# Row-centred output weights, and a sum of squares on ScalarE, for the two output LayerNorms of an attention and slot-mixture kernel

## What is computed

```python
def _layernorm(x, axis=-1, eps=1e-05):
    m = jnp.mean(x, axis=axis, keepdims=True)
    v = jnp.var(x, axis=axis, keepdims=True)
    return (x - m) / jnp.sqrt(v + eps)
...
x = x + _layernorm(_L0_attn_ref(_layernorm(x), ...))   # ends in  out @ Wo + bo
x = x + _layernorm(_L0_ffn_ref(_layernorm(x), ...))    # ends in  out @ c_Wo + c_bo
```

## Time and profile before

| | |
|---|---|
| median of 3 runs | 501.3 us (497.4 to 502.04) |
| the profiled execution, its own time | 501.44 us |
| its span, first to last instruction | 499.4 us |
| PE busy, of the span | 403.0 us (81%) |
| DVE busy | 308.8 us (62%) |
| ACT busy | 232.0 us (46%) |
| POOL busy | 149.2 us (30%) |
| mean granted TensorE clock | 0.919 |

### The profile page before, as it was taken

One profiled execution on the slowest core, in us unless ns is written; L12 is line 12 of the kernel. 1 busy time (PEld: TensorE's weight loads), 2 busy tenths in 40 slices (PEclk: granted clock), 3 DMA queues, 4 the chain that ended last, 5 costly groups with the idle time before them and its releaser, 6 DMA issues.

```text
span 499.4 us, 6939 instructions
## 1 busy us (share of the span) xinstructions
PE 403.0 (81%) x2072; PEld 249.7 (50%) x2072; DVE 308.8 (62%) x1177; ACT 232.0 (46%) x422; POOL 149.2 (30%) x253
## 2 busy tenths in 40 slices
PE   3876657569799955759899999999996679999981
PEld 3533223225455532545677675834442326888871
DVE  4599999979995948253542534333332214969984
ACT  2326646747768656456765564200000001356765
POOL 3105554465755350311330220010000000335453
PEclk9997887979799977688999999999998879999997
DMA  4293011001010261217545676639999999801223
GB/s 146 81 315 107 1 43 42 19 24 43 1 42 3 74 252 43 78 53 266 209 148 174 219 233 219 257 140 402 387 399 388 397 378 354 266 0 43 84 86 126
DMA packets 43599, 81.69 MB, mean 164 GB/s; under 512 B 1831, under 2 KB 36269, under 8 KB 39085
## 3 DMA queue, kind: packets, MB, share of 16 engines
q1 hardware_dynamic: 42504, 80.05, 45.7%
q10 hardware_dynamic: 1060, 1.22, 0.8%
HBM read 69.73 MB, written 11.53 MB: 163 GB/s over the span
## 4 chain that ended last, share of the span: by engine, by line
PE 53%; DVE 20%; ACT 8%; issue 5%; SPq 5%; DMA 4%; POOL 3%; DVEq 1%; POOLq 0%; ACTq 0%
PE bank L1469 6%; PE bank L1445 6%; PE bank L1112 5%; PE bank L1078 5%; PE bank L1141 5%; PE bank L1045 4%; DVE top L1608 4%; SPq L403 4%; PE bank L1358 4%; DMA x<-in_L_ffn_e_W_dram 3%; PE bank L1067 3%; DVE exc L1639 2%; DVE stats L1533 2%; PE bank L1057 2%; PE bank L1388 2%
## 5 line engine op out<-in xcount | busy, mean ns | idle before, releaser
L1045 PE MATMUL bank<-Wz,yT 128*128 128x512 f32 x128 | 70.7, 704 | 24.2 <-DVE top L1608 21.6
L1045 PEld LDWEIGHTS bank<-Wz,yT 128*128 128x128 f32 x128 | 28.2, 229 | 60.4 <-issue 49.2
L1608 DVE MAX8 top<-bank 128x8 f32<-128x32 f32 x512 | 51.5, 180 | 4.1 <-ACT scr L727 2.4
L979 ACT ACTIVATE d<-d 128x32 f32<-128x32 f32 x16 | 3.7, 229 | 92.1 <-DVE d L1959 92.1
L1078 PE MATMUL bank<-aWo,hoT 128*128 128x256 f32 x128 | 39.4, 434 | 3.5 <-DVE arena L1727 3.5
L568 POOL TENSOR_SCALAR veps<-mv 128x4 f32<-128x4 f32 x24 | 5.7, 237 | 110.4 <-DVE mv L1536 83.3
L675 POOL TENSOR_TENSOR work<-work 128x512 f32<-128x512 f32 x16 | 16.6, 1060 | 64.7 <-DVE work L2024 64.7
L1727 DVE TENSOR_TENSOR arena<-bank,Wz 128x256 f32<-128x256 f32 x16 | 6.7, 418 | 45.1 <-PE bank L1078 45.1
L706 ACT ACTIVATE arena<-arena,shift,rstd 128x256 f32<-128x256 f32 x64 | 33.2, 596 | 2.6 <-POOL shift L690 2.6
L1067 PE MATMUL bank<-heads 128*64 128x256 f32 x128 | 22.9, 437 | 11.4 <-issue 5.8
L1078 PEld LDWEIGHTS bank<-aWo,hoT 128*128 128x128 f32 x128 | 23.7, 205 | 14.1 <-issue 10.2
(11 more groups left out here) (256 smaller groups left out, 877.9 us busy)
## 6 DMA issues: line engine op xcount, KB each, us to landing
x<-in_L_ffn_e_W_dram SPq DMA_DIRECT2D x9, 1024.0 KB, 9.9
arena<-in_L_ffn_e_W_dram SPq DMA_DIRECT2D x9, 1024.0 KB, 13.8
scr<-in_L_ffn_e_W_dram SPq DMA_DIRECT2D x8, 1024.0 KB, 14.6
arena<-in_L_ffn_e_Wg_dram SPq DMA_DIRECT2D x6, 1024.0 KB, 6.9
work<-in_L_ffn_e_W_dram SPq DMA_DIRECT2D x5, 1024.0 KB, 8.4
xin<-in_L_attn_query_dram SPq DMA_DIRECT2D x8, 512.0 KB, 4.1
x<-in_L_attn_query_dram SPq DMA_DIRECT2D x1, 4096.0 KB, 16.5
out_dram<-x SPq DMA_DIRECT2D x8, 512.0 KB, 3.2
```

What stands on the lines that cost most here:

```text
L1045: mm = pe.matmul(bZ[t % 2][:, :], yT[:, c, t * P:(t + 1) * P], Wz[:, c, :], start=(c == 0), stop=(c == C - 1))
L1608: mx = v.max(top[:, h * TG + t, :], bZ[t % 2][:, h * NS:(h + 1) * NS])
```

## The change

The columns of the output weights `aWo` and `cWo` and of the output biases are centred once: from each row of 256 values its mean is taken away. The projection then has mean zero over its 256 outputs, so the norm needs the mean square alone, and no shift.
- ACT centres with `centre_rows`, two activations for each row block, the second of which waits for the first: `aWo` (two blocks) and `cbo` right after the loop over groups 0 and 1, ahead of `clamp(2)`; `abo` ahead of `signs(7, 1)`; `cWo` (two blocks) after the experts' last Silu. DVE centres `bo3` with three small instructions ahead of `split3`.
- `output_statistics` and `norm_out` (DVE), `norm_o` and `apply_out` (ACT) go. For the first batch ACT follows each `take_o(n)` by a Square of the tile with a sum over the row; in the last stage `square_out(j)`, four Squares, follows `put_out(j)`. Each Square waits for the one before it and for ACT's own copy. The second batch's heads keep DVE's statistics.
- The Square of the first tile of a group waits in addition for POOL to have read the sums of the group before: `vare[1]` at g.
- POOL's `roots(1, g)` and `out_roots` have two instructions where they had four.
- `join` and `add_stream` have one SCALAR_TENSOR_TENSOR for each tile (scale times output plus x) where one TENSOR_TENSOR added the whole group, and wait for POOL in place of ACT.

```diff
+                if k == 1 and i < GB:
+                    pool.tensor_scalar(veps[:, k, :], osq[:, :], 1.0 / D, EPS, ALU.mult, ALU.add).then_inc(vare[k], 1)
+                else:
+                    pool.tensor_scalar(veps[:, k, :], mv[:, k, :, 1], EPS, None, ALU.add).then_inc(vare[k], 1)
+                if k == 1:
+                    pool.wait_ge(vare[k], i + 1)
+                    pool.tensor_tensor(rstd[:, k, :], veps[:, k, :], mhalf[:, :], ALU.pow).then_inc(rst[k], 1)
+                    return
...
                 act.activation(o[:, g % 2, n % TG, :], psO, ACT.Copy).then_inc(o_sb, 1)
-
-            def norm_o(g, tiles=range(TG)):
-                act.wait_ge(rst[1], g + 1)
-                for t in tiles:
-                    scaled(1, t, o[:, g % 2, t, :], o[:, g % 2, t, :]).then_inc(o_norm, 1)
+                if n % TG == 0 and g >= 1:
+
+                    act.wait_ge(vare[1], g)
+                if n > 0:
+                    act.wait_ge(mean[1], n)
+                act.wait_ge(o_sb, n + 1)
+                act.activation(unread[:, :], o[:, g % 2, n % TG, :], ACT.Square, accum_out=osq[:, n % TG:n % TG + 1])\
+                    .then_inc(mean[1], 1)
+
+            def centre_rows(k, rows_, idle):
+
+                act.activation(idle, rows_, ACT.Identity, scale=-1.0 / D, accum_out=centre[:, k:k + 1]).then_inc(summed, 1)
+                act.wait_ge(summed, k + 1)
+                act.activation(rows_, rows_, ACT.Identity, bias=centre[:, k:k + 1]).then_inc(centred, 1)
...
+            act.wait_ge(w_in1, 16 * N_W1)
+            act.wait_ge(bo_in, 32)
+            for c in range(C):
+                centre_rows(c, aWo[:, c, :], hoT[:, 0, :, :].rearrange("p m n -> p (m n)"))
+            centre_rows(2, cbo[:, :], hoT[:, 0, :, :].rearrange("p m n -> p (m n)"))
             clamp(2)
...
             take_o(15)
+            act.wait_ge(abo_in, 16)
+            centre_rows(3, abo, Wz[:, 0, D:2 * D])
             signs(7, 1)
...
+            act.wait_ge(w_in3, 16 * N_W3)
+            for c in range(C):
+                centre_rows(4 + c, cWo[:, c, :], y[:, 2, :])
...
+            def square_out(j):
+                k0 = next(k for k, p in enumerate(portions) if p[0] == j)
+                for t in range(TG):
+                    k = k0 if t < portions[k0][2] else k0 + 1
+                    if k >= 3 and t == portions[k][1]:
+
+                        act.wait_ge(c_vare, k - 2)
+                    if j * TG + t > 0:
+                        act.wait_ge(c_mean, j * TG + t)
+                    act.wait_ge(co_sb, j * 2 + (t // 2 + 1))
+                    act.activation(unread[:, :], co[j % CO][:, t, :], ACT.Square, accum_out=csq[:, k % 3, t:t + 1])\
+                        .then_inc(c_mean, 1)
...
                 put_cpT(j)
-                if j >= 2:
-                    apply_out(j - 2)
                 put_out(j)
-            for k in range(NG - 2, len(portions)):
-                apply_out(k)
+                square_out(j)
...
             def join(g):
-                v.wait_ge(o_norm, g * TG + TG)
-                tiles = x[:, g * TG:(g + 1) * TG, :]
-                v.tensor_tensor(tiles, tiles, o[:, g % 2, :, :], ALU.add).then_inc(x_new, 1)
+                v.wait_ge(rst[1], g + 1)
+                for t in range(TG):
+                    tile = x[:, g * TG + t, :]
+                    x_ = v.scalar_tensor_tensor(out=tile, in0=o[:, g % 2, t, :], scalar=rstd[:, 1, t:t + 1], in1=tile,
+                                                op0=ALU.mult, op1=ALU.add)
+                x_.then_inc(x_new, 1)
```

More of the change, by code:

```diff
@@ L124, in build @@
         cbo = sb("cbo", [P, D])
+        centre = sb("centre", [P, 6])
+        osq = sb("osq", [P, TG])
+        csq = sb("csq", [P, 3, TG])
+        unread = sb("unread", [P, D], BF16)
         stats = sb("stats", [P, 3, TG, 6])
@@ L225, in build @@
         bo_in = sem("bo_in")
+        summed = sem("summed")
+        centred = sem("centred")
         w_in2 = sem("w_in2")
@@ L683, in out_roots @@
                 if k >= 3:
[L684 to L690, removed]
+                    hold(c_out, k - 2)
+                pool.tensor_scalar(veps[:, w, lo:hi], csq[:, w, lo:hi], 1.0 / D, EPS, ALU.mult, ALU.add).then_inc(c_vare, 1)
+                pool.wait_ge(c_vare, k + 1)
+                pool.tensor_tensor(rstd[:, w, lo:hi], veps[:, w, lo:hi], mhalf[:, lo:hi], ALU.pow).then_inc(c_rst, 1)
             weigh(0, 0)
@@ L921, in _ @@
             put_slot_scores(1)
-            norm_o(2)
             take_h(15)
@@ L961, in _ @@
             second_norm(6)
-            norm_o(7)
             put_norm(6)
@@ L1013, in _ @@
             put_out(0)
+            square_out(0)
             for j in range(1, NG):
@@ L1074, in project @@
                     pe.wait_ge(o_sb, n)
+                else:
+                    pe.wait_ge(centred, C)
                 if n < KT:
@@ L1425, in fold_values @@
             def fold_values(b):
+                pe.wait_ge(centred, 6)
                 for m in range(2):
@@ L1714, in check @@
                 v.tensor_copy(flag[:, :], moved[:, 0:1]).then_inc(settled, 1)
[L1716 to L1722, removed]
             def keep_output(n):
@@ L1847, in _ @@
             v.wait_ge(bo_in, 32)
+            bsum = centre[0:3, 4:5]
+            own(v.tensor_reduce(bsum, bo3, AX_X, ALU.add))
+            own(v.tensor_scalar(bsum, bsum, 1.0 / D, None, ALU.mult))
+            own(v.tensor_scalar(bo3, bo3, bsum, None, ALU.subtract))
             own(split3(ab3[:, :], bo3))
@@ L1891, in _ @@
             check(1)
-            output_statistics(3)
             group_maximum(1)
-            v.wait_ge(abo_in, 16)
+            v.wait_ge(centred, 4)
             for n in range(KT + 2, 2 * KT + 2):
@@ L2024, in total @@
                     v.reciprocal(crs[:, half], csum[:, half]).then_inc(c_rs, 1)
[L2026 to L2039, removed]
-                    v.bn_aggr(mv[:, w, t, :], stats[:, w, t, :]).then_inc(c_mean, 1)
             def add_stream(k):
@@ L2044, in add_stream @@
                 v.wait_ge(back[j % 2], 16 * (j // 2 + 1))
-                v.wait_ge(c_norm, j * TG + hi)
-                tiles = co[j % CO][:, lo:hi, :]
-                v.tensor_tensor(tiles, tiles, x[:, j * TG + lo:j * TG + hi, :], ALU.add).then_inc(c_out, 1)
+                v.wait_ge(c_rst, k + 1)
+                for t in range(lo, hi):
+                    tile = co[j % CO][:, t, :]
+                    c_ = v.scalar_tensor_tensor(out=tile, in0=tile, scalar=rstd[:, k % 3, t:t + 1], in1=x[:, j * TG + t, :],
+                                                op0=ALU.mult, op1=ALU.add)
+                c_.then_inc(c_out, 1)
             soften(0, 0)
```

19 lines of the change are left out of this document (1 added, 18 removed).

## The result

Slower, as forecast, and by somewhat more. The changed kernel has a median of 510.8 us (507.5 to 511.0, 4 runs) beside 499.4 us for the kernel before on the same chip, a ratio of 1.023 [1.018, 1.028]. A second series gave 510.9 us (508.4 to 512.8, 6 runs) beside 497.6 (17 runs), 1.026 [1.023, 1.029]. I had said 509, from +8.0 on the profiled execution's 501.44. The profiled executions differ by 9.2 us (510.61 and 501.44; spans 508.8 and 499.4); the medians differ by 11 to 13, since that profiled execution lay near the upper end of the kernel before's runs (495.7 to 503.2 in all series).

The account below looks back on a forecast made before the run. It took ACT as the awaited engine early on and PE as busy throughout from 425 to 475 us. +5.3 us up to 290 us and +2.7 in the last stage made +8.0 on 501.44: 509 us, 8-in-10 range 501 to 516.

Parts of the forecast that it names:

- (1): Ahead of clamp(2): three centring pairs on ACT lie on the path, +2.9 us (2.1 to 3.4).
- (2): bo3 centred on DVE, about 1.1 us: hidden by DVE's wait for ACT's scores, 0; +1.1 without that cover.
- (8): cWo centred on ACT after the last Silu, 1.9 us: hidden behind PE's remaining work, 0.
- (3): First batch's heads: DVE's saved statistics gain 0; Squares of tiles 3, 8 and 13 delay awaited work, +0.6, +0.6, +0.5 us.
- (4): Tile 12's Square waits for POOL on vare[1]: ACT stands still 5 us and take_o(13) ends later, +0.5 us.
- (6): Joins 0 to 7 each take 0.3 us longer; joins 1, 2, 4 and 6 are on the path, +1.2 us.
- (7): norm_o(3) gone: join(3) starts 1.3 us sooner but takes 0.3 more, -1.0 us; later norm_o's gone give 0.
- (9): Last stage: rounds 8.01 us for 7.78, +1.15; outputs(6) and outputs(7) +2.2 each; end -2.8; sum +2.7 us.
- A: Rival: ACT's Squares cost nearly nothing, 0.35 us each with overlap kept, giving 504.4 us; chance 0.15.
- B: Rival: DVE's relief at the four output_statistics counts, 7.2 us off the path, giving 496.5 or 494 us; chance 0.09.
- C: Rival: PE's pauses drop the granted clock for a tenth of the last stage's 75 us, 7 us more, 516 us; chance 0.12.
- D: Rival: Square needs another activation table, 18 us or more of loads in the last stage, 527 us; chance 0.04.

Follow-up runs that it names:

- experiment 2: Kernel before with only the last stage changed (square_out after put_out) and cWo and cbo centred after the last Silu: 503.16 us, ratio 1.006.
- experiment 8: Kernel before with only the last stage's change, square_out(j - 1) after put_cpT(j), last group's first two Squares between put_out's halves: 493.04 us, ratio 0.992.
- experiment 10: Kernel of experiment 8 plus 8 idle matmuls ahead of the products of experts 11 to 15: 493.53 us, ratio 0.993 to the kernel before.
- experiment 3: Changed kernel with square_out(j - 1) moved behind put_cpT(j), same instructions: 503.54 us, ratio 1.010 to the kernel before.
- experiment 5: The changed kernel timed again, unaltered, as measure for other runs: 510.9 us, ratio 1.026 to the kernel before.
- experiment 6: Changed kernel with 12 idle matmuls ahead of outputs(6) and 9 ahead of outputs(7): 508.88 us, ratio 1.023 to the kernel before.
- experiment 9: Changed kernel with 8 idle matmuls ahead of the products of experts 11 to 15: 508.05 us, ratio 1.020 to the kernel before.
- experiment 7: Changed kernel with aWo and cbo centred early, Squares behind put_cpT, and two sets of sums avoiding the POOL wait: 502.36 us, ratio 1.010 to the kernel before.
- experiment 1: Changed kernel with the last stage, cWo and cbo as before, so the first norm's half alone: 505.96 us, ratio 1.014 to the kernel before.
- experiment 4: Changed kernel with aWo and cbo centred between put_yT(0) and norm_y(1), ahead of the loop: 509.37 us, ratio 1.020 to the kernel before.
- experiment 11: Changed kernel with the three centring pairs ahead of clamp(2) made twice: 513.68 us, ratio 1.033 to the kernel before.
- experiment 12: Changed kernel with two sets of sums, so tile 12's Square no longer waits for POOL: 510.05 us, ratio 1.024 to the kernel before.

## Why the prediction was right, point by point

The direction and the places were right; up to 290 us the terms come to +5.2 for +5.3 once traces of like clock are compared, and the clock, which I had kept as a rival, made part of the time behind. For the heads every trace is cut at the same matmuls of PE; times that name a stretch are those of the kernel before.

A profiled pair alone doesn't price them. The kernel before and experiments 2, 8 and 10 run the same program up to the experts, and so do the changed kernel and experiments 3, 5, 6 and 9. And executions of one program still differ: at the matmul that ends the gathering the first four stand at 288.26, 288.55, 288.80 and 283.81 us, the other five at 291.87, 294.49, 293.21, 290.16 and 290.48. So the 3.6 us of the profiled pair there is one draw, and what an edit costs has to be read between traces whose granted clock is the same in that stretch (numbers in brackets are those of experiments, "all ten" with the half counts the changed kernel):

| stretch, and what is in it | without the first norm's half | with it | difference |
|---|---|---|---|
| 64.1 to 80.5, centring | 16.44 (before) | 19.26 (experiment 3); 16.44 where it is moved (7) | +2.82 |
| 110.2 to 131.8, tile 3, clock 1.00 | 21.60 (before, 2, 8) | 22.20 (3, 7) | +0.60 |
| the same, low clock in the first 3 to 4 us | 21.17 (10) | 21.77 (1, 4, 6, 9) | +0.60 |
| 213.9 to 218.9, `join(3)` | 4.97 (all four) | 4.00 (all ten) | -0.97 |
| 237.9 to 242.0, `join(4)` | 4.14 (all four) | 4.59 (1, 6, 9, 11) | +0.45 |
| 259.9 to 288.3, `join(6)` | 28.37 (all four) | 28.80 (all ten) | +0.43 |

The clock in two of these pairs: windows (us; PE, PEld, DVE, ACT, POOL busy; clock; DMA share, GB/s) of the kernel before and of experiment 3, which was 0.6 us later up to 71 us and has 0.57 from 67.6 to 71.6 us as the kernel before has from 67 to 71:

```profile
74.00:78.00 4.00, 3.31 (x5) 1.55 (x6) 3.54 (x23) 3.97 (x5) 2.88 (x5) 0.57 0.00 0
110.00:132.00 22.00, 18.31 (x86) 10.55 (x86) 21.28 (x118) 15.69 (x29) 13.41 (x13) 1.00 0.08 25
```

```profile
74.60:78.60 4.00, 3.29 (x5) 1.53 (x6) 2.13 (x22) 3.90 (x12) 2.90 (x5) 0.57 0.00 0
114.00:136.00 22.00, 18.08 (x84) 10.27 (x81) 21.29 (x118) 16.96 (x36) 13.40 (x13) 1.00 0.09 25
```

(1) Centring, +2.9: 2.82 us at 0.94 for a pair (I had 0.95), and experiment 11 and the first row of the table show it on the path. In the profiled run only 1.8 show at 80 us, since the clock from 65 to 75 us happened to be higher than before (1.00 against 0.74 and 0.84).

(2), (5) and (8), priced at nothing, cost nothing that the traces show; for `cWo` experiment 2 shows it, while no run has (2) or (5) alone.

(3) The Squares in the heads, forecast +0.6, +0.6 and +0.5. Tile 3's costs its 0.60 (table). The profiled pair can't show it: the ten traces with the half spread from 21.77 to 22.72 us there with the clock. Tile 8's and `join(1)` show at the end of their stage: 170 to 182 us takes 11.55 us in the four kernels without that half and 12.61 to 12.63 in all ten with it, +1.07 where I had +0.9. Ahead of `clamp(7)` the Square takes its 0.42 us behind `take_o(13)`.

(4) The wait for POOL, +0.5: 0.1 (experiment 12). The mechanism was exact, a stop of 5.90 us where I had said 5; I had set too much work behind it.

(6) The joins: 0.45 us longer each, not 0.3 (1.67 against 1.22). From 182 to 202 us, where tile 13's Square, the wait and `join(2)` together were +1.3, the traces have 21.15 against 20.33, +0.8.

(7) `norm_o(3)` gone, -1.0, with `join(4)` and `join(6)`, +0.6: -0.4 forecast for 202 to 288 us. By the table it is -0.97 + 0.45 + 0.43, so -0.1: the gain was exact, the joins longer. The whole stretch shows the clock more than this: it takes 87.8 us in the changed kernel and 87.0 to 87.8 in experiments 3, 4, 5, 7 and 12, 84.8 to 85.3 in experiments 1, 6, 9 and 11, and 85.9 in the kernel before, but 85.1 in experiment 10. The first six have a granted clock of 0.83 from 240 to 250 us, and all others 1.00. Windows of the changed kernel and of experiment 9:

```profile
240.00:250.00 10.00, 8.11 (x38) 6.07 (x39) 4.77 (x19) 5.17 (x9) 3.96 (x10) 0.83 0.30 118
```

```profile
240.00:250.00 10.00, 7.93 (x47) 5.82 (x47) 5.01 (x20) 6.19 (x12) 3.96 (x10) 1.00 0.57 208
```

Without what the clock did, (1) to (7) thus come to 2.8 + 0.6 + 1.1 + 0.8 - 0.1 = +5.2, for +5.3. The changed kernel's own trace has +3.6 at 288 us, from larger pieces of both signs: 132 to 142 us took 7.2 us in place of 9.9, at a clock that had been low before (0.83 from 130 to 150 us) and was 1.00, while 110 to 130 us had the lower clock now.

**The step that fell** is the sentence behind the sum, that the experts carry the delay on undiminished. The weights do carry it (3.6 became 3.1), but the last expert then ran at half clock for most of its length, +2.4 us, and in experiment 9, with PE kept busy ahead of it, these 2.4 us are gone.

(9) The last stage, +2.7. Rounds: 7.95 for 8.01, and 0.7 for 1.15 in all. `outputs(6)`: +2.1 for 2.2. `outputs(7)`: +3.7 for 2.2, of which 1.7 is the clock behind the pause of 3.35 us (experiment 6). The end: 4.6 us for 4.4 (the last `put_out` ends at 501.53, DVE at 506.17). Sum +3.9. A Square every 0.54 us was as priced.

**The rivals.** A (Squares nearly free) is out by that 0.54. B (DVE's relief counts) is out: 6.21 us of waiting became 8.64. C named the right mechanism in too wide a form: the rounds kept 1.00 (25 us of them, from 456 on), and in this stage only the one long pause cost 1.7 us. D is out: the trace still has three table loads, of 1283 ns, and Squares stand between Exp and Copy without one. The Trainium skill, "ScalarE: Activation LUTs", section "Table sets: the hidden batching unit", names no square among the functions that are in every set; in this kernel it went with Exp, Copy and Sign.

**The sum.** 3.6 to 290 us (5.3 forecast), -0.5 and +2.4 in the experts, +3.9 in the last stage (2.7): 9.4. That the total came near the forecast is in part luck of this pair: at 290 us 1.6 of the 5.2 us don't show in it, and in the last expert the clock took 2.4.

By the medians the whole change costs 11 to 13 us, 2 to 4 more than in the profiled pair; the runs of one kernel differ by 1 to 7 us, and only one of each has a trace. The 4.8 us that experiment 7 left by the medians are of that kind in the main. Its trace has +1.1 in the last expert (3.23 us for the 16 products), +0.6, +1.07 and +0.7 in the heads and +1.7 from 202 to 288 us, but nothing for the centring, -1.9 from 132 to 142 us, where the clock of the kernel before was low, and an end 2.9 us shorter; its profiled execution is only 0.5 us above that of the kernel before (501.97 and 501.44), whose median beside it was 497.6. There is no trace of such a short run of the kernel before, but one of experiment 10, the same program up to the experts, and it reaches the end of the gathering 4.5 us sooner (283.81 for 288.26).

**What stays open:** why the last expert's clock is low in the nine traces with the first norm's half and no idle matmuls there, and in none of the three without that half. The pause right ahead of it doesn't decide it: it was 1.34 to 1.60 us in three of the nine, and 2.06 in the kernel before. Open, too, is why six traces have the low clock from 240 to 250 us and the others don't.

## What to carry to other kernels

When work is moved from one engine to another, ask at each place which engine the next wait ends on; a total of busy time freed (here over 20 us on two engines) says nothing. Put new work behind what another engine waits for, not ahead of it: the same Squares cost 6.5 to 8 us in one place, and nothing in the rounds behind the `put_cpT` that PE waited for. And look at what a pause of PE does to the matmuls behind it, since a wait of 2 us more cost 1.7 us on top. Last, one program's executions stood up to 5 us apart at the same matmul here, so a profiled pair can't price an edit of that size: compare stretches between traces whose granted clock is the same in them.

## What the runs showed that I had not expected

- The granted clock after a single pause: the 16 matmuls of `outputs(6)` took 3.72 us behind a pause of 1.33 or 1.34 us and 5.41 behind one of 3.35, the first in six traces, the second in seven (5.35 in one of them); behind a pause filled with idle matmuls, one every 0.22 us, 3.72 again.
- A sum over the row costs an activation little: 0.42 us for 256 values, the accumulator's read of 0.19 begins 0.10 to 0.11 before it ends, and the next dependent Square starts 0.54 after the last. The first Square, which also waits for ACT's own copy, began at 453.10, before the 0.60 of that copy had run out (453.20).
- Four SCALAR_TENSOR_TENSOR on 256 values in a row take 1.67 us, 0.38 to 0.40 apart, but 2.56 us where the first two (0.57 and 1.27 us) ran beside POOL's multiplications of `weigh` (once, from 489.47 in the changed kernel; POOL's two took 2.25 us there in place of 2.07).
